# One-hots of q for a sort's lookups: TensorE transposes, or a VectorE comparison on bytes spread by DMA

## The chip, the cores and the metric

The kernel runs on one core of one Trainium2 chip. The metric is the device time of one execution in microseconds (us): less is better. Engines: PE is TensorE (PEld its weight loads), DVE is VectorE, ACT is ScalarE, POOL is GpSimd, SP is SyncE; a "q" behind a name (SPq) is the engine's queue.

## The reference

Two graph layers over 3,125 nodes of 128 features and 100,000 edges, with float32 in and out:

```
# layer 0: every edge sends h[dst] + edge_attr @ W_edge + b_edge to node src
h    = x @ W_lin + b_lin
aggr = segment_sum(h[dst] + (edge_attr @ W_edge + b_edge), src, 3125)
x    = layernorm(x + relu(aggr))
# layers of the second block, three times: mean over the edges of one (dst, type), 8 types
msg  = u[src];  seg = dst * 8 + type
h    = segment_sum(msg, seg) / max(count(seg), 1)
u    = einsum('nrf,rfo->no', h.reshape(n, 8, f), W) + u @ root + bias     # relu between them
out  = layernorm(x + u)
```

In the kernel the message of the second block is made at the edge's source and added at its destination. For that the edges are brought into an order by cells: a cell is a pair of q (the window of 128 destination nodes and the upper two bits of the type: Q = 100 values) and f (the source window and the type's last bit: F = 50 values).

## The kernel before

The stages, with their places in the profiled execution:

- 0 to 105 us: edges are loaded as a tile of 128 partitions x COLS = 784 columns. DVE and PE work out for each edge a row in DRAM (`slot_rows`), sorted by the window of src.
- 105 to 314 us: a histogram of the cells. DVE makes one-hots of q and f (`pick_qf`, L1232 in `pick_of`), PE multiplies them (`count_group`), and DVE turns the counts into start positions of the cells.
- 314 to 1356 us: the sort. 49 groups of GC = 16 columns (GROUPS = 49), each of GB = 4 steps of four columns; 196 steps. Two more groups only place.
- From about 1356 us: gathers, window sums, and the three layers. The change doesn't touch them.

Beside the first stages and most of the sort POOL scatters the edge rows to DRAM: EC = 98 chunks of CH = 8 indirect DMAs, 784 in all (L609). ACT builds each chunk in one of NB = 4 buffers (`build_rows`: it waits until the chunk four before has been scattered and landed). LEAD = 18 chunks are built ahead of the sort; then ACT builds two at the start of each of the first BUILDS = 40 groups (g0 from 0 to 39 in `rank_group`). The order on each engine is written out by hand, and engines meet only in semaphores.

One step n of the sort (column c of four; `sort_group` on PE, `rank_group` on ACT, `sort_picks` on DVE):

- PE, `turn_q(n + 1)`: four transposes of the q one-hots of the next step into the PSUM tile `QT` (100 x 512, float16; L895), then four of the 13 key bits into `BITS_T` (L897).
- ACT, `copy_bits` and `copy_q`: these two tiles go to SBUF, q as float32 into `pick_qT`, double buffered. All ACT copies have line L644.
- PE, for each column: `permute` of an older column (two matmuls of 500 columns, L806), then `look_up` (L809): the turned one-hot `pick_qT` picks from `table` (100 x 50, float32) the next free position of each edge's cell, and an `add` counts the column in. ACT copies the new table to SBUF for the next column (`copy_table`): a chain from PE to ACT and back, four times in a step.
- PE, `pair_keys(n + 1)`: which edges of a column have the same key (L904 and four L806); ACT `copy_same` takes it.
- DVE: `pick_place` makes four one-hots of 1000 (L1416; eight buffers, so it waits for the permute eight columns back), `take_looked(n - 1)` (L1386) takes what was looked up, `place` works out positions, and `pick_ranked` and `pick_dst` make the next group's one-hots (L1232).

`q_h` holds the q of each edge as float16 (128 partitions x 784 columns). What `look_up` needs turned is, for each of four columns, a 100 x 128 matrix with a one where q of the edge in that partition equals the row.

```
            def turn_q(n, par, c0):
                wait_used(pe, S["q_copied"], n)
                for c in range(4):
                    nc.tensor.transpose(QT[:, P * c:P * (c + 1)], column(pick_q[par], c0 + c), ident_h[:, :])
```

Of the kernel before, what the change touches and what calls it, by code (L numbers as in the profile page):

```python
# [24 lines left out]
F32 = mybir.dt.float32  # L25
F16 = mybir.dt.float16
BF16 = mybir.dt.bfloat16
I32 = mybir.dt.int32
# [5 lines left out]
P = 128  # L34
# [9 lines left out]
def ds(start, size):  # L44
    return bass.ds(start, size)


def gnn_resnorm(nc, x, src, dst, edge_attr, edge_type, W_lin, b_lin, W_edge, b_edge, W1, root1, b1,
# [62 lines left out]
    with ctx:  # L111
# [8 lines left out]
        slot_rows = nc.dram_tensor("slot_rows", [SLOTS + NW * P + COLS, PAY], F32).ap()  # L120
        slot_blocks = slot_rows.rearrange("(b r) f -> b (r f)", r=P // ZB)
        msgs = nc.dram_tensor("msgs", [SLOTS_A, D], F32).ap()
        msg_blocks = msgs.rearrange("(b k) f -> b (k f)", k=BLK)
# [79 lines left out]
        more_hi = [words(y_sb, at + b * HI // 2, HI // 2, BF16) for b in range(4)]  # L203
        at += 2 * HI
        pairs_at = 2 * HALF - 2 * P
        block_j, block_r = words(y_sb, pairs_at - 2 * NS, NS), words(y_sb, pairs_at - NS, NS)
# [54 lines left out]
        def take(size, dt=F32):  # L261
# [71 lines left out]
        DVE_BANKS = ACC // 2 + 1  # L333
        QT = ps[0:Q, 4, 0:256].bitcast(F16)
        BITS_T = ps[0:KEYBITS, 4, 256:512].bitcast(F16)
# [12 lines left out]
                 "qf_picked d_picked turned_q bits_copied q_copied paired same_made looked_up "  # L348
                 "column_counted table_copied mult_made columns_used lo_picked hi_picked perm_used "
                 "sort_done slots_made slots_used idx_made "  # L350
# [9 lines left out]
        gathered = [[sem(f"gathered{i}_{half}") for half in range(2)] for i in range(NB)]  # L360
        stored = [sem(f"stored{i}") for i in range(4)]
        b_gathered = [sem(f"b_gathered{i}") for i in range(RB)]

# [275 lines left out]
        def _(act):  # L639
# [33 lines left out]

            def copy_q(n, q):
                copy(pick_qT[:, q, :], QT).then_inc(S["q_copied"], 1)

# [4 lines left out]
            def rank_group(g, par, pair, g0):  # L681
                if g0 < BUILDS:
                    for q in range(2):
                        turn = LEAD + 2 * par + q
                        build_rows(2 * g + (LEAD + q), q, g + LEAD // 2, turn % NB, pair + turn // NB)
                for b in range(GB):
                    n = GB * g + b
                    ahead = g0 < GROUPS - 1 or b < GB - 1
                    copy_table(4 * n, 0)
                    if ahead:  # L690
                        copy_bits(n + 1, (b + 1) % 2)
                    copy_table(4 * n + 1, 1)
                    if ahead:
                        copy_q(n + 1, (b + 1) % 2)
                    copy_table(4 * n + 2, 0)
                    copy_table(4 * n + 3, 1)
                    if ahead:
                        copy_same(n + 1, (b + 1) % 2)

            copy_bits(0, 0)  # L700
            copy_q(0, 0)
            copy_same(0, 0)
# [88 lines left out]
        def _(pe):  # L791
# [55 lines left out]

            clear((2,))

            def count_group(g, par, n):  # L850
# [23 lines left out]
            for rh in range(BLK):  # L874
# [3 lines left out]
                m.then_inc(S["a_counted"], 1)  # L878
            pe.wait_ge(S["b_started"], 1)
            whole(ps[:, 4, 0:NS], ones[0:Q, :], started_b).then_inc(S["b_counted"], 1)  # L880
            for f in range(F):
# [10 lines left out]
            def turn_q(n, par, c0):  # L892
                wait_used(pe, S["q_copied"], n)
                for c in range(4):
                    nc.tensor.transpose(QT[:, P * c:P * (c + 1)], column(pick_q[par], c0 + c), ident_h[:, :])  # L895
                for c in range(4):
                    m = nc.tensor.transpose(BITS_T[:, P * c:P * (c + 1)], bits_st[:, par, c0 + c, :],  # L897
                                            ident_h[:, :])
                m.then_inc(S["turned_q"], 1)
# [204 lines left out]
        def _(dve):  # L1104
# [115 lines left out]
            bits(key2[:, :], raw[:, 2, :], 1, ALU.arith_shift_right)  # L1220
            then(v.scalar_tensor_tensor(q_h[:, :], key[:, :], 4.0, key2[:, :], ALU.mult, ALU.add))
            bits(key2[:, :], raw[:, 2, :], 1, ALU.bitwise_and)
# [15 lines left out]
            def pick_qf(g, par, done):  # L1238
                pick_of(pick_q[par], in_pairs(q_h[:, ds(g * GC, GC)]), Q)
                pick_of(pick_f[par][:, :, 0:F, :], in_pairs(f_h[:, ds(g * GC, GC)]), F).then_inc(S[done], 1)  # L1240

            def pick_hist(g, par, n):
# [134 lines left out]
            def pick_dst(g, par, half):  # L1377
# [3 lines left out]
                if half:  # L1381
                    m.then_inc(S["d_picked"], 1)

            def take_looked(n, b, par):
                dve.wait_ge(S["looked_up"], n + 1)
# [33 lines left out]
            def sort_picks(g, par, pair, g0):  # L1419
                for b in range(GB):  # L1420
# [6 lines left out]
                    if b and g0 < GROUPS:  # L1427
                        take_looked(GB * g + (b - 1), b - 1, par)
                    if b == 0 and 1 <= g0 <= GROUPS:
                        place(g - 1, 1 - par)  # L1430
# [7 lines left out]
                    if b >= 2 and g0 < GROUPS - 1:  # L1438
                        pick_dst(g + 1, 1 - par, b - 2)

            pick_ranked(0, 0)
            for half in range(2):
# [216 lines left out]
```

## Time and profile before

| | |
|---|---|
| median of 3 runs | 4906.59 us (4905.39 to 4911.11) |
| the profiled execution: time | 4906.83 us |
| the profiled execution: span, first to last instruction | 4905.1 us |
| outside the span | 1.7 us |
| mean granted TensorE clock | 0.905 |
| busy, share of span | PE 82%, DVE 69%, POOL 49%, ACT 44% |

How the profile is read: busy times are sums over an execution in which the stages have different limits. "Idle before" is the time in which an engine waited just before an instruction, and the name behind the arrow is what it waited for. A granted clock of 1.00 is TensorE's full 2.4 GHz, 0.50 is 1.2 GHz. Durations of neighbouring instructions of one engine can overlap a little.

### The profile page before, as it was taken

Reading aid. Unit: us, or ns where it says so; the run is one execution under the profiler, and the core shown is the slowest. Engines: PE = TensorE matmul, PEld = TensorE weight load, DVE = VectorE, ACT = ScalarE, POOL = GpSimd, SP = SyncE. Lnnn points to the kernel's source line nnn. Section 1 sums busy time; section 2 is a strip of 40 time slices with the busy share of each in tenths; the row PEclk is TensorE's granted clock in tenths of the full one; section 3 lists DMA queues with packets and bytes.
Section 4 is the critical chain, followed back from the end, with each engine's and each line's share of the span. In section 5 each row is a group of like instructions: output and inputs, shape, how many; then the busy total and the mean of one; then the engine's idle time right before and its main releaser. Section 6 shows DMA issues by size and latency. Waiting matters only on the chain.

```text
span 4905.1 us, 118298 instructions
## 1 busy us (share of the span) xinstructions
PE 3998.8 (82%) x30835; PEld 3134.4 (64%) x30836; DVE 3368.4 (69%) x8053; ACT 2159.3 (44%) x5004; POOL 2391.5 (49%) x2369
## 2 busy tenths in 40 slices
PE   3589888889956666666688889989889999888997
PEld 2456655656645554455457777776777776777776
DVE  8858777778877777777656665665665765666666
ACT  0025555555511111111145556765555775555675
POOL 2877777776067777777500005750002772000575
PEclk9559989889977888888789999999999999999999
DMA  1111111111033333333315556754555773555676
GB/s 43 39 43 55 46 51 48 48 51 30 0 97 77 78 77 77 78 77 76 51 43 171 170 170 188 208 169 124 172 172 168 208 209 103 172 172 172 189 209 180
DMA packets 672517, 553.37 MB, mean 113 GB/s; under 512 B 158723, under 2 KB 584885, under 8 KB 672462
## 3 DMA queue, kind: packets, MB, share of 16 engines
q0 software_dynamic: 111712, 277.47, 20.3%
q1 hardware_dynamic: 560750, 275.24, 19.3%
q8 instruction: 25, 0.41, 0.0%
q14 instruction: 30, 0.25, 0.0%
HBM read 307.55 MB, written 244.94 MB: 113 GB/s over the span
## 4 chain that ended last, share of the span: by engine, by line
PE 49%; POOL 24%; issue 16%; DVE 5%; DMA 5%; DVEq 1%; ACT 1%; POOLq 0%; ACTq 0%; SPq 0%
PE ps L809 25%; PE ps L806 17%; POOL slot_rows L609 11%; POOL y_sb L620 10%; PE ps L1065 4%; DMA mid<-msgs,block_idx 3%; POOL mid L632 3%; DMA y_sb<-in_x_dram,idx_st 1%; DVE mid L1531 1%; DVE y_sb L1262 0%; PE ps L897 0%; DVE y_sb L1232 0%; PE ps L1031 0%; DVE mid L1605 0%; PE ps L895 0%
## 5 line engine op out<-in xcount | busy, mean ns | idle before, releaser
L632 POOL DMA_INDIRECT mid<-msgs,block_idx x750 | 715.4, 954 | 1745.2 <-DMA msgs<-mid 1498.6
L644 ACT ACTIVATE mid<-ps 128x512 f32<-128x512 f16 (+4 forms) x2484 | 1083.8, 464 | 1023.1 <-PE ps L1065 298.9
L806 PE MATMUL ps<-mid 128*128 128x128 f32 (+3 forms) x7668 | 1236.1, 300 | 88.7 <-DMA mid<-msgs,block_idx 31.6
L806 PEld LDWEIGHTS ps<-mid 128*128 128x128 f32 (+3 forms) x7668 | 857.5, 175 | 318.7 <-issue 263.9
L809 PE MATMUL ps<-y_sb,mid 128*128 x6552 | 946.4, 288 | 132.8 <-issue 130.4
L620 POOL DMA_INDIRECT y_sb<-in_x_dram,idx_st x808 | 795.3, 984 | 413.3 <-issue 246.4
L609 POOL DMA_INDIRECT slot_rows<-y_sb,row_st x784 | 863.2, 1101 | 270.5 <-issue 236.9
L809 PEld LDWEIGHTS ps<-y_sb,mid 128*128 128x128 f32 x6552 | 794.7, 191 | 258.7 <-issue 211.7
L1605 DVE TENSOR_SCALAR mid<-iota,slot_lo,slot_w 128x128 f32<-128x128 f32 x2250 | 663.1, 378 | 313.9 <-PE ps L806 304.1
L809 PE MATMUL ps<-y_sb 128*128 128x193 f32 x1616 | 423.5, 417 | 291.3 <-DVE mid L1531 187.3
L644 ACT ACTIVATE y_sb<-ps 128x512 bf16<-128x512 f16 (+2 forms) x375 | 205.0, 554 | 1007.1 <-PE ps L986 877.2
L1596 DVE COPY mid<-ps 128x512 f32<-128x512 f32 x411 | 284.9, 693 | 482.2 <-PE ps L809 482.2
L809 PEld LDWEIGHTS ps<-mid 100*128 100x128 f32 (+2 forms) x1884 | 351.4, 208 | 388.7 <-ACT mid L644 213.7
L809 PE MATMUL ps<-mid 100*128 100x50 f32 (+2 forms) x1884 | 444.7, 329 | 145.8 <-ACT mid L644 90.0
L809 PEld LDWEIGHTS ps<-y_sb 128*128 128x128 f32 x1616 | 346.9, 244 | 310.9 <-DVE mid L1531 240.4
L1588 DVE TENSOR_TENSOR mid<-iota_h,a_code 128x512 f16<-128x512 f16 x819 | 525.6, 684 | 0.0
L806 PE MATMUL ps<-y_sb 128*100 128x50 f16 (+2 forms) x3886 | 494.8, 250 | 12.6 <-DVE y_sb L1232 12.6
L644 ACT ACTIVATE mid<-zeros,slot_w 128x128 f32<-128x128 f32 x750 | 371.2, 495 | 205.1 <-PE ps L806 168.4
L1531 DVE TENSOR_TENSOR mid<-mid,ps 128x193 f32 x808 | 286.8, 355 | 199.1 <-PE ps L809 71.2
L644 ACT ACTIVATE zeros<-iota,zeros 128x128 f32<-128x128 f32 x750 | 300.8, 401 | 106.2 <-DMA msgs<-mid 11.5
L1416 DVE TENSOR_SCALAR mid<-iota_h,mid 128x1000 bf16<-128x1000 f16 x392 | 213.0, 562 | 161.6 <-PE ps L806 159.1
L1065 PE MATMUL ps<-ident_h,mid 128*128 128x128 f16 x3276 | 318.0, 220 | 4.8 <-DVE mid L1588 4.6
(244 smaller groups left out, 3743.5 us busy)
## 6 DMA issues: line engine op xcount, KB each, us to landing
msgs<-mid SPq DMA_DIRECT2D x819, 256.0 KB, 2.3
y_sb<-slot_rows SPq DMA_DIRECT2D x101, 268.0 KB
y_sb<-in_edge_attr_dram SPq DMA_DIRECT2D x54, 256.0 KB
y_sb<-in_x_dram,idx_st POOLq DMA_INDIRECT x808, 2.5
slot_rows<-y_sb,row_st POOLq DMA_INDIRECT x784
mid<-msgs,block_idx POOLq DMA_INDIRECT x750, 3.7
y_sb<-in_edge_attr_dram SPq DMA_DIRECT2D x44, 224.0 KB
mid<-in_L_gnn_W_dram SPq DMA_DIRECT2D x3, 512.0 KB
```

The costliest lines, as they stand in the source:

```text
L609: nc.gpsimd.indirect_dma_start(out=slot_rows, out_offset=bass.IndirectOffsetOnAxis(ap=row_st[:, b, k:k + 1], axis=0), in_=stage[:, b, PAY ...
L620: nc.gpsimd.indirect_dma_start(out=slots[b][:, k, 0:D], out_offset=None, in_=x, in_offset=bass.IndirectOffsetOnAxis(ap=idx_st[:, b, k:k + ...
L632: nc.gpsimd.indirect_dma_start(out=rows[:, s % RB, :], out_offset=None, in_=msg_blocks, in_offset=bass.IndirectOffsetOnAxis(ap=block_idx[: ...
L644: return nc.scalar.activation(o, i, func, **kw)
L806: return nc.tensor.matmul(o, a, b, start=False, stop=False, skip_group_check=True)
L809: return nc.tensor.matmul(o, a, b, start=True, stop=True, skip_group_check=True)
L1065: t = nc.tensor.transpose(A_TRN[par][:, P * k:P * (k + 1)], a_sel[:, b, k, :], ident_h[:, :])
L1416: v.tensor_scalar(pick_hi[ci % 8], iota_h[:, 0:HI], hi_f[:, par, ci:ci + 1], mult[:, ds(c, 1)], ALU.is_equal, ALU.mult).then_inc(S["hi_pic ...
L1531: v.tensor_tensor(to, to, ps[:, (k // 2) % 2, SUM * (k % 2):SUM * (k % 2 + 1)], ALU.add).then_inc(S["tile_added"], 1)
L1588: v.tensor_tensor(a_sel[:, b, :, :], iota1_h[:, :].unsqueeze(1).to_broadcast([P, BLK, P]), a_code[:, ds(g * BLK, BLK)].unsqueeze(2).to_bro ...
L1596: v.tensor_copy(a_out[:, b, :], ps[:, 2 + b, :]).then_inc(S["a_taken_dve"], 1)
L1605: m = v.tensor_scalar(b_sel[:, b % 2, k, :], iota[:, 0:P], slot_lo[:, ds(s * BLK + k, 1)], slot_w[:, ds(s * BLK + k, 1)], ALU.is_equal, AL ...
```

## The change

The turned one-hots `pick_qT` are no longer made by PE and copied by ACT, but compared by DVE.

- Once, ahead of the histogram: PE transposes all of `q_h` in seven transposes (`Q_TURNED`, PSUM bank 4), DVE writes it as bytes (`q_st`) in two instructions, and ACT stores it to a DRAM tensor `q_codes`, one row of 128 bytes for each column of edges.
- For each step: ACT issues one DMA (`load_q`) that reads the 512 bytes of the step's four columns and writes them to each of 100 partitions (`q_row`, four buffers, issued three steps ahead, in the place in ACT's order where `copy_q` stood).
- For each step: DVE (`turned_q`, behind `take_looked`) compares the 100 x 512 bytes with the partition's number and writes `pick_qT` as float32.
- PE's transposes of q in `turn_q` and ACT's `copy_q` go. `turn_q` waits for `bits_copied` in place of `q_copied`.

```diff
+        q_codes = nc.dram_tensor("q_codes", [QTILES * P, P], U8).ap()
+        q_steps = q_codes[0:COLS, :].rearrange("(n i) p -> n (i p)", i=4)
...
-            def copy_q(n, q):
-                copy(pick_qT[:, q, :], QT).then_inc(S["q_copied"], 1)
+            def load_q(n, b):
+
+                wait_used(act, S["q_copied"], n - 3)
+                act.dma_start(q_row[b], q_steps[ds(n, 1), :].to_broadcast([Q, 4 * P])).then_inc(q_in[b], 16)
...
                     copy_table(4 * n + 1, 1)
-                    if ahead:
-                        copy_q(n + 1, (b + 1) % 2)
+                    if g0 < GROUPS - 1 or b < GB - 3:
+                        load_q(n + 3, (b + 3) % 4)
                     copy_table(4 * n + 2, 0)
...
+            act.wait_ge(S["q_staged"], 2)
+            act.dma_start(q_codes[0:(QTILES - 1) * P, :].rearrange("(t c) p -> c t p", c=P),
+                          q_st[:, 0:(QTILES - 1) * P].rearrange("c (t p) -> c t p", p=P)).then_inc(S["q_stored"], 16)
...
+            act.wait_ge(S["q_stored"], 32)
+            for n in range(3):
+                load_q(n, n)
             copy_bits(0, 0)
-            copy_q(0, 0)
...
             clear((2,))
+            pe.wait_ge(S["q_coded"], 1)
+            for t in range(QTILES):
+                n = min(P, COLS - t * P)
+                m = nc.tensor.transpose(Q_TURNED[0:n, t * P:(t + 1) * P], q_h[:, t * P:t * P + n], ident_h[:, :])
+            m.then_inc(S["q_turned"], 1)
...
             def turn_q(n, par, c0):
-                wait_used(pe, S["q_copied"], n)
-                for c in range(4):
-                    nc.tensor.transpose(QT[:, P * c:P * (c + 1)], column(pick_q[par], c0 + c), ident_h[:, :])
+                wait_used(pe, S["bits_copied"], n)
...
+            dve.wait_ge(S["q_turned"], 1)
+            whole_q = (QTILES - 1) * P
+            v.tensor_scalar(q_st[:, 0:whole_q], Q_TURNED[:, 0:whole_q], 1.0, None, ALU.mult).then_inc(S["q_staged"], 1)
+            rest_q = (slice(0, COLS - whole_q), slice(whole_q, whole_q + P))
+            v.tensor_scalar(q_st[rest_q], Q_TURNED[rest_q], 1.0, None, ALU.mult).then_inc(S["q_staged"], 1)
...
+            def turned_q(n, b, turn):
+
+                wait_used(dve, S["looked_up"], n - 1)
+                dve.wait_ge(q_in[b], 16 * turn + 16)
+                v.tensor_scalar(pick_qT[:, b % 2, :], q_row[b], part[0:Q, 0:1], None, ALU.is_equal
+                                ).then_inc(S["q_copied"], 1)
...
                         take_looked(GB * g + (b - 1), b - 1, par)
+                    if g0 < GROUPS - 1 or (g0 < GROUPS and b < GB - 1):
+                        turned_q(GB * g + (b + 1), (b + 1) % 4, g + (b + 1) // 4)
...
+            turned_q(0, 0, 0)
             pick_ranked(0, 0)
```

## Rows read from the trace of the kernel before

**Rows 1.** The page: the chain that ended last, by engine.
```profile
PE 49%; POOL 24%; issue 16%; DVE 5%; DMA 5%; DVEq 1%; ACT 1%; POOLq 0%; ACTq 0%; SPq 0%
```
**Rows 2.** The chain of waits in time, 300 to 1360 us: shares by line.
```profile
by line: POOL slot_rows L609 51.6%; issue 16.6%; PE ps L806 16.6%; PE ps L809 6.4%; PE ps L897 1.9%; PE ps L895 1.7%; PE ps L904 1.5%; ACT mid L644 0.5%; ACT y_sb L644 0.5%; PE ps L802 0.4%; POOLq L606 0.2%; POOLq L396 0.2%; DMA slot_rows<-
```
**Rows 3.** Windows of the sort: length, busy PE, PEld, DVE, ACT, POOL (xcount), PE clock, DMA.
```profile
450.00:700.00 250.00, 221.87 (x2089) 149.94 (x2088) 191.33 (x384) 129.57 (x392) 194.52 (x183) 0.90 0.17 48
1166.00:1183.40 17.40, 16.88 (x144) 11.65 (x144) 11.79 (x21) 8.83 (x28) 13.74 (x13) 0.80 0.09 26
1183.40:1200.70 17.30, 17.30 (x182) 11.87 (x180) 16.22 (x34) 9.77 (x29) 13.64 (x13) 1.00 0.08 24
1218.00:1322.00 104.00, 104.00 (x1080) 71.69 (x1080) 93.15 (x199) 58.94 (x168) 0.00 (x0) 1.00 0.00 0
```
**Rows 4.** ACT's wait for the chunk four before, at a group's start (timeline).
```profile
1165.53 0.75 ACT L644 ACTIVATE y_sb<-y_sb 128x512 f32<-128x512 f32 x2 [4.01 <-DMA slot_rows<-y_sb,row_st]
```
**Rows 5.** DVE's waits (total us, times, longest) and `copy_q`, 1218 to 1322 us.
```profile
DVE y_sb L1416 <- PE ps L806: 5.7, 12, 0.8
DVE mid L1416 <- PE ps L806: 4.3, 18, 0.4
L644 ACT ACTIVATE mid<-ps 100x512 f32<-100x512 f16 x24 | 14.2, 591 | 0.0
```
**Rows 6.** The timeline of one step at full clock: start, us, engine, line.
```profile
604.25 0.41 PE L895 MATMUL ps<-ident_h,y_sb 128*100 128x128 f16 x4
604.59 0.39 PE L897 MATMUL ps<-ident_h,y_sb 128*13 128x128 f16 x4
605.02 1.68 ACT L644 ACTIVATE mid<-ps 13x512 f16<-13x512 f16 x4 [0.55 <-PE ps L897]
607.24 0.41 PEld L809 LDWEIGHTS ps<-mid 100*128 100x128 f32 x2
```
**Rows 7.** DVE, lines by form, 0 to 320 us: forms near the added ones.
```profile
L1343 DVE TENSOR_SCALAR mid<-iota,mid 100x128 f32<-100x128 f32 x50 | 15.0, 299 | 16.0 <-PE ps L806 16.0
L1194 DVE TENSOR_SCALAR mid<-mid,start_col 25x808 f32<-25x808 f32 x1 | 0.6, 629 | 0.0
L1252 DVE TENSOR_SCALAR mid<-mid 128x784 int32<-128x784 int32 x1 | 0.6, 569 | 0.0
L1187 DVE TENSOR_SCALAR mid<-ps 128x784 int32<-128x784 f32 x1 | 1.0, 976 | 1.5 <-PE ps L806 1.5
```
**Rows 8.** Scatters of POOL beside DVE instructions (timeline).
```profile
196.28 1.31 POOL L609 DMA_INDIRECT slot_rows<-y_sb,row_st  x1 [0.30 <-issue]
262.90 0.29 DVE L1343 TENSOR_SCALAR mid<-iota,mid 100x128 f32<-100x128 f32 x1 [0.48 <-PE ps L806]
263.09 0.97 POOL L609 DMA_INDIRECT slot_rows<-y_sb,row_st  x1 [0.30 <-issue]
263.10 0.41 DVE L1344 TENSOR_SCALAR mid<-mid 100x250 f32<-100x250 f32 x1
605.12 1.21 DVE L1232 TENSOR_TENSOR y_sb<-y_sb,mid 128x2048 f16<-128x2048 f16 x1
605.61 1.56 POOL L609 DMA_INDIRECT slot_rows<-y_sb,row_st  x1 [0.30 <-issue]
```
**Rows 9.** The start of the histogram and of the sort (timeline).
```profile
110.11 2.97 PE L806 MATMUL ps<-y_sb 128*100 128x50 f16 x32 [5.63 <-DVE y_sb L1232]
318.06 0.63 PE L895 MATMUL ps<-ident_h,y_sb 128*100 128x128 f16 x4
319.26 1.06 ACT L644 ACTIVATE mid<-ps 13x512 f16<-13x512 f16 x2 [39.04 <-PE ps L897]
323.31 0.97 POOL L609 DMA_INDIRECT slot_rows<-y_sb,row_st  x1 [3.94 <-ACT row_st L644]
```
**Rows 10.** Issues on SP's queue (timeline), and a time to landing (DMA view).
```profile
322.67 1.09 SPq L493 DMA_DIRECT2D y_sb<-in_edge_attr_dram  x2
...
slot_rows<-zeros SPq DMA_DIRECT2D x1, 871.0 KB, 6.1
```

More of the change, by code:

```diff
@@ L26 @@
 F16 = mybir.dt.float16
+U8 = mybir.dt.uint8
 BF16 = mybir.dt.bfloat16
@@ L121, in gnn_resnorm @@
         slot_blocks = slot_rows.rearrange("(b r) f -> b (r f)", r=P // ZB)
+        QTILES = -(-COLS // P)
+        q_codes = nc.dram_tensor("q_codes", [QTILES * P, P], U8).ap()
+        q_steps = q_codes[0:COLS, :].rearrange("(n i) p -> n (i p)", i=4)
         msgs = nc.dram_tensor("msgs", [SLOTS_A, D], F32).ap()
@@ L204, in gnn_resnorm @@
         at += 2 * HI
+        q_at = COLS * KEYBITS // 2 + COLS // 2
+        q_row = [words(y_sb, q_at + b * P, P)[0:Q, :].bitcast(U8) for b in range(4)]
+        q_st = words(y_sb, q_at + 4 * P, QTILES * P // 4).bitcast(U8)
+        assert q_at + 4 * P + QTILES * P // 4 <= SORT_AT
         pairs_at = 2 * HALF - 2 * P
@@ L333, in gnn_resnorm @@
         DVE_BANKS = ACC // 2 + 1
-        QT = ps[0:Q, 4, 0:256].bitcast(F16)
+        Q_TURNED = ps[:, 4, 0:QTILES * P // 2].bitcast(F16)
         BITS_T = ps[0:KEYBITS, 4, 256:512].bitcast(F16)
@@ L348, in gnn_resnorm @@
                  "qf_picked d_picked turned_q bits_copied q_copied paired same_made looked_up "
-                 "column_counted table_copied mult_made columns_used lo_picked hi_picked perm_used "
+                 "q_coded q_turned q_staged q_stored column_counted table_copied mult_made columns_used lo_picked hi_picked perm_used "
                  "sort_done slots_made slots_used idx_made "
@@ L361, in gnn_resnorm @@
         stored = [sem(f"stored{i}") for i in range(4)]
+        q_in = [sem(f"q_in{i}") for i in range(4)]
         b_gathered = [sem(f"b_gathered{i}") for i in range(RB)]
@@ L698, in rank_group @@
                         copy_same(n + 1, (b + 1) % 2)
+            act.wait_ge(S["q_staged"], 2)
+            act.dma_start(q_codes[0:(QTILES - 1) * P, :].rearrange("(t c) p -> c t p", c=P),
+                          q_st[:, 0:(QTILES - 1) * P].rearrange("c (t p) -> c t p", p=P)).then_inc(S["q_stored"], 16)
+            rest = COLS - (QTILES - 1) * P
+            act.dma_start(q_codes[COLS - rest:COLS, :], q_st[0:rest, (QTILES - 1) * P:QTILES * P]
+                          ).then_inc(S["q_stored"], 16)
+            act.wait_ge(S["q_stored"], 32)
+            for n in range(3):
+                load_q(n, n)
             copy_bits(0, 0)
-            copy_q(0, 0)
             copy_same(0, 0)
@@ L879, in _ @@
             pe.wait_ge(S["b_started"], 1)
+            pe.wait_ge(S["q_staged"], 2)
             whole(ps[:, 4, 0:NS], ones[0:Q, :], started_b).then_inc(S["b_counted"], 1)
@@ L1220, in _ @@
             bits(key2[:, :], raw[:, 2, :], 1, ALU.arith_shift_right)
-            then(v.scalar_tensor_tensor(q_h[:, :], key[:, :], 4.0, key2[:, :], ALU.mult, ALU.add))
+            v.scalar_tensor_tensor(q_h[:, :], key[:, :], 4.0, key2[:, :], ALU.mult, ALU.add).then_inc(S["q_coded"], 1)
+            dve.wait_ge(S["q_coded"], 1)
             bits(key2[:, :], raw[:, 2, :], 1, ALU.bitwise_and)
```

## The prediction

> **What bounds the kernel now.** I began with the chain that ended last: PE 49%, POOL 24% [rows 1]. The change touches one stage of it, so the next view was the chain in time over the sort: the scatters of L609 carry 51.6% of it, and most of the 16.6% "issue" is the gap of 0.30 us behind each of them [rows 2, 8]. PE stands there with under 30%. The windows tell where. From 450 to 700 us POOL is busy for 194.52 of 250 us with 183 scatters, so one comes every 1.366 us and the 16 that belong to a group take 21.9 us; PE has its clock at 0.90 [rows 3]. At a group's start ACT waits up to 4.01 us for a chunk that POOL has only just scattered, and everyone behind ACT waits with it [rows 4]. The last such wait ends at 1165.53. From there on PE is the bound: 104.00 us busy of 104.00, at full clock, and `copy_q`, which runs once a step, has run 24 times: 4.333 us a step, 17.33 a group [rows 3, 5]. So a group costs PE 17.33 us, and in the first 40 groups POOL needs more than that. What the sort's engines gain there is waited away; a gain on PE counts in group 39 and in the nine behind it.
>
> And DVE is close behind PE: in the same 104 us it waited for PE only 5.7 + 4.3 = 10.0 us, 0.417 a step [rows 5]. Its own work, gaps and overlaps counted, is 4.333 - 0.417 = **3.916 us a step**.
>
> **What goes.** The four q transposes of a step take PE from 604.25 to 604.59: 0.34 us at full clock [rows 6], about 0.6 at half clock (0.63 at 318.06) [rows 9]. PE alone would then step in 3.99 us. ACT's copy of q is one of the four in the 1.68 us behind `copy_bits` [rows 6]. It delays nobody today: the third table copy ends with that row at 606.70, and PE loads for that lookup at 607.24. So its going brings nothing.
>
> **What comes on DVE.** `turned_q` is a compare with a per-partition scalar, 100 x 512, float32 out, 196 times. The trace has no byte input. Nearest is L1343 (100 x 128, the same compare, float32): 0.299 us in the mean; L1194 has 808 elements in 0.629 [rows 7]. The slope is 0.330/680 = 0.485 ns an element, so 512 give 0.299 + 384 x 0.000485 = 0.485 us. Neighbours on DVE overlap (L1343 starts at 262.90, lasts 0.29, and the next starts at 263.10) [rows 8] by 0.09, so it takes 0.40 us of DVE's time. The other end is half that rate: of the same 784 elements, L1187 takes 0.976 us where L1252 takes 0.569, 0.52 ns more an element [rows 7]; for 512 that gives 0.75 us, 0.67 of DVE's time. I take 0.40, since L1343 does the same operation with the same output. By the Trainium skill (VectorE: DVE Perf Modes, "What auto-detection actually checks") a single source with source and target in SBUF gets two elements a cycle whatever the type; no row here shows it for bytes.
>
> DVE's step becomes 3.916 + 0.40 = **4.316 us**, against PE's 3.99 and today's 4.333. The bound moves from PE to DVE and the step stays as it is. This is the core of the forecast. Its two new waits hold nothing: `looked_up` was just waited for by `take_looked`, and the bytes were asked for three steps ahead, 13 us, where 871 KB land in 6.1 us [rows 10]. If they did hold, `pick_ranked` and the one-hots for `permute` stand behind them on DVE, and PE waits for those. PE's own wait for `pick_qT` has slack: DVE makes it right behind `take_looked`, whose wait ends as PE starts the step before the one that needs it.
>
> **What comes on ACT.** One DMA issue a step in the place of a copy. Two issues on SP's queue with an address from a register took 1.09 us, 0.55 each [rows 10]; the copy took 0.591 [rows 5]. Up to 0.54 us more than the copy (from 606.70 to 607.24), that is to about 1.1 us, the issue delays nobody.
>
> **Start.** DVE's byte writes stand ahead of the histogram, which DVE paces: L1187 (PSUM, 784 elements) took 0.976 [rows 7], so 768 take about 0.96, the 16 x 128 rest 0.29, less overlap: +1.1 us (at two elements a cycle +0.7). PE's seven transposes, some 1.1 us at half clock by 0.63 for four, lie in its wait of 5.63 us [rows 9]; without this cover they would cost that 1.1. Store and first loads lie in ACT's wait of 39.04 us, and POOL stands still for 3.94 us until the first chunk is built [rows 9], so a late sort start counts in full. On that path q's transposes at 318.06 go: -0.6. The first `turned_q` (0.4) is hidden: PE clears banks until 318.06 and comes to the one-hots only then [rows 9]. Start: **+0.5 us**.
>
> **Groups 0 to 38.** DVE's 1.6 us more and PE's 1.4 less a group both disappear in POOL's 21.9: **0**, if a scatter stays as long as it is.
>
> **Groups 39 to 48.** Group 39 starts at half clock with DVE rested (11.79 busy of 17.40) [rows 3]: PE's gain, 0.6 + 2 x 0.34, -1.3. In groups 40 and 41 POOL still runs and DVE is slower, 16.22 us busy in the first against 93.15/6 = 15.53 later [rows 3]: twice 17.26 + 0.69 - 17.33 at most, and less in the second: +1.1. Groups 42 to 47: 24 x -0.017 = -0.4. Group 48 has no next group's one-hots to make, so PE is the bound, with three sets of transposes less: -1.0. Sum **-1.6**; I add 1 us for hand-overs between two engines that are both about 90% busy or more.
>
> The sum: 4906.83 + 0.5 + 0 - 1.6 + 1.0 = 4906.7, **4907 us**. It is made against the profiled execution (span 4905.1 and 1.7 around it), which lies 0.2 us above the median.
>
> **Rivals.**
>
> *PE's gain is kept.* DVE's work with the compare stays under PE's 3.99 us a step, because its instructions run closer together when it never waits; of the 0.40 added only 3.99 - 3.916 = 0.07 may show. Then groups 40 to 48 run at 3.99: 35 x 0.34 = 11.9, against nothing in the forecast but group 48's 1.0 and the 0.7 around it. 4906.83 + 0.5 - 1.3 - 11.9 = 4894. Against it: DVE is 90% busy already [rows 3], and the smaller compare L1343 alone takes 0.299. For it: DVE's 3.916 us are worked out from waits, not from rows of each gap.
>
> *POOL's scatters get longer (slower).* Place: the 156 steps of the POOL-bound groups 0 to 38. A scatter takes 0.97 alone, but 1.56 where an L1232 of 1.21 us (two SBUF inputs) covers its start, and 1.31 beside float and integer instructions of 0.57 us [rows 8]. `turned_q` stands between L1386 and, in three steps of four, an L1232. If it costs a scatter half of 0.34 us, that is 156 x 0.17 = 27: 4934. It decides from 0.063 us each (9.8/156). Against it: beside L1343 and L1344, which share operation, scalar and output type with it, the scatter at 263.09 stays at 0.97 [rows 8]. The Trainium skill (GPSIMD Engine Reference, "Key points") says that VectorE instructions in a two-port mode contend with GpSimd for SBUF; L1343 at two elements a cycle would be one, and that scatter doesn't show it; the one at 605.61, under a two-input L1232, does. The order in time of scatters and L1232 shifts too, either way: a scatter takes 194.52/183 = 1.063 in the mean, 0.09 over 0.97, some 56 us in 39 groups of 16, and a tenth of it is 6.
>
> *A byte costs one element a cycle.* DVE's step is 3.916 + 0.67 = 4.586, 0.253 over today's in 32 steps: +8.1. With +1.1, +0.5, -1.3 and 1 for hand-overs: 4916.
>
> *The bytes come late or ACT's issue exceeds 1.1 us*, so that lookups wait: the change then isn't the prefetch it says. At 1.5 us an issue PE would step in 4.4: +3 over ten groups, inside the forecast's range.
>
> **How the numbers follow.** The forecast, with the last rival in it: 0.57, its own range 4899 to 4917 (6 us for the scatters' order, 2 for the start, 2 for hand-overs, either way). PE's gain kept: 0.16. Scatters longer: 0.17. Bytes at one a cycle: 0.10. The range leaves out most of the scatters' rival and a little on the fast side: 4892 to 4926. A measurement of this kernel can tell 0.2%, 9.8 us, from no change. Faster by more: 0.16 and a tail of 0.01, 0.17. Slower: 0.15, 0.05 of the byte rival and 0.02: 0.22. Between: 0.61.
>
> **What the profile after would show.** Right: in the window of the last groups DVE without waits and PE with some 0.3 us of idle a step; steps of 4.3 us; scatters' mean between 1.05 and 1.09; the last of ACT's waits for a chunk ending within 8 us of 1165.5. Wrong: `turned_q` far from 0.48 us; scatters of 1.2 us beside it; DVE's waits for PE as before; PE's clock below 1.00 in the last groups.

## The result

The changed kernel takes 5018.95 us (median of 4 runs, 5015.75 to 5022.51), the kernel before 4908.85 in the same runs: a ratio of 1.0226, 95% interval 1.0213 to 1.0239. The forecast was 4907, its range ended at 4926, so it missed by 112 us. The profiled execution has a span of 5020.8 us, 115.7 over the span before.

Scatters over the whole profile, first before (L609) and then after (L618): count, busy us, mean ns, idle before them.

```profile
L609 POOL DMA_INDIRECT slot_rows<-y_sb,row_st x784 | 863.2, 1101 | 270.5 <-issue 236.9
```
```profile
L618 POOL DMA_INDIRECT slot_rows<-y_sb,row_st x784 | 1004.0, 1281 | 263.9 <-issue 237.5
```

The same 784 scatters, with the same gap of 0.30 us behind each (236.9 and 237.5 us of "issue" in all), are busy for 140.8 us more. The windows after show where; the first answers the first of [rows 3], the second the last of [rows 3] (columns as there).

```profile
450.00:700.00 250.00, 191.56 (x1612) 128.48 (x1610) 172.54 (x366) 91.47 (x296) 201.84 (x159) 0.82 0.18 51
...
1333.00:1437.00 104.00, 102.95 (x1026) 68.54 (x1025) 103.39 (x230) 49.19 (x151) 9.10 (x5) 1.00 0.06 14
```

In 250 us POOL gets through 159 scatters instead of 183, so one comes every 1.572 us where it was 1.366, and a group of 16 takes 25.2 us, not 21.9. PE does less in that time and its granted clock is 0.82 instead of 0.90. In the last groups it is as forecast: DVE, busy for 103.39 of 104 us, is the bound, and PE has idle time at full clock.

ACT's last wait for a chunk, which ended at 1165.53 [rows 4], now ends here:

```profile
1289.68 0.75 ACT L653 ACTIVATE y_sb<-y_sb 128x512 f32<-128x512 f32 x2 [4.66 <-DMA slot_rows<-y_sb,row_st]
```

That is 124.2 us later. The sort's result is copied out at 1472.3 where it was 1356.0, 116.3 us later. So all of the loss, and 7.9 us more, arises in the groups that POOL bounds, and the last groups give 7.9 back.

**One scatter.** The timeline of DVE and POOL in step 1 of a group, before (start, us, engine, line):

```profile
709.26 1.22 DVE L1232 TENSOR_TENSOR mid<-y_sb,mid 128x2048 bf16<-128x2048 f16 x1
709.46 1.85 POOL L609 DMA_INDIRECT slot_rows<-y_sb,row_st  x1 [0.30 <-issue]
710.39 0.21 DVE L1374 COPY y_sb<-y_sb 128x208 f16 x1
710.51 1.47 DVE L1232 TENSOR_TENSOR y_sb<-y_sb,mid 128x1600 f16<-128x1600 f16 x2
711.62 1.21 POOL L609 DMA_INDIRECT slot_rows<-y_sb,row_st  x1 [0.30 <-issue]
```

The scatter ends at 711.31, 0.83 us behind the end of the first one-hots (710.48), though the copy and two more follow: at that boundary it got in. The same place after:

```profile
616.15 0.37 DVE L1423 TENSOR_TENSOR mid<-ps,y_sb 128x204 f32<-128x204 f32 x1
616.44 0.48 DVE L1418 TENSOR_SCALAR mid<-y_sb,part 100x512 f32<-100x512 uint8 x1
616.83 1.22 DVE L1256 TENSOR_TENSOR mid<-y_sb,mid 128x2048 bf16<-128x2048 f16 x1
616.94 3.46 POOL L618 DMA_INDIRECT slot_rows<-y_sb,row_st  x1 [0.30 <-issue]
617.96 0.21 DVE L1404 COPY y_sb<-y_sb 128x208 f16 x1
618.09 1.47 DVE L1256 TENSOR_TENSOR y_sb<-y_sb,mid 128x1600 f16<-128x1600 f16 x2
```

Here it ends at 620.40, 0.84 us behind the end of the *last* one-hots (619.56). It was kept out through the whole chain: one-hots of the low digit, copy of the bits, one-hots of q and f. A third scatter, in steps 2 and 3, where no chain follows:

```profile
622.11 1.21 DVE L1256 TENSOR_TENSOR y_sb<-y_sb,mid 128x2048 f16<-128x2048 f16 x1
622.20 1.96 POOL L618 DMA_INDIRECT slot_rows<-y_sb,row_st  x1 [0.30 <-issue]
```

It started 0.09 us behind the one-hots and took 1.96; the one at 605.61 started 0.49 behind them and took 1.56 [rows 8]. Both end 0.84 us after the one-hots do. The 0.40 us between them are what the compare moved the one-hots by.

So there are two effects, and I have taken the sum over all scatters from 323 us to the last one (640 single ones before, 641 after), each less 0.967, a free one's duration. Before, 69.7 us; after, 206.1.

- 42 scatters take more than 2.25 us, 99.9 us over a free one in all, 2.38 each. Before there is none; at 0.60 each (the mean of those of 1.4 to 2.25 us before) they would be 25. The chains' hold: 75 us.
- 78 take 1.4 to 2.25 us, 0.99 each over a free one, against 0.60: 30 us.
- Together that is 120 scatters held by one-hots, before it was 71: 49 more, at 0.60: 29 us. The rest is 2.

What holds them was open here: the compare, the loads, or the order of things.

### The profile page after: what moved, and what is told of

The parts are those of the page before. It is cut to its first block, busy times and chain, and to the rows that moved or that the text cites. A ratio compares the mean times of both kernels' runs of the same rounds, so it can differ in the third digit from the quotient of the medians.

```text
span 5020.8 us, 117371 instructions
## 1 busy us (share of the span) xinstructions
PE 3976.7 (79%) x30058; PEld 3110.5 (62%) x30059; DVE 3424.7 (68%) x8251; ACT 2064.4 (41%) x4808; POOL 2532.2 (50%) x2369
## 4 chain that ended last, share of the span: by engine, by line
PE 45%; POOL 27%; issue 16%; DMA 5%; DVE 5%; DVEq 1%; ACT 0%; POOLq 0%; SPq 0%; ACTq 0%
PE ps L828 24%; PE ps L825 15%; POOL slot_rows L618 15%; POOL y_sb L629 10%; DMA mid<-msgs,block_idx 4%; PE ps L1088 4%; POOL mid L641 2%; DMA y_sb<-in_x_dram,idx_st 1%; DVE mid L1645 0%; DVE y_sb L1292 0%; DVE mid L1571 0%; DVE y_sb L1256 0%; PE ps L1054 0%; PE ps L1107 0%; DVE y_sb L1532 0%
## 5 line engine op out<-in xcount | busy, mean ns | idle before, releaser
L653 ACT ACTIVATE mid<-ps 128x512 f32<-128x512 f16 (+4 forms) x2288 | 988.1, 453 | 1123.7 <-PE ps L825 450.2
L825 PE MATMUL ps<-mid 128*128 128x128 f32 (+3 forms) x7668 | 1257.0, 303 | 92.1 <-DMA mid<-msgs,block_idx 33.8
L618 POOL DMA_INDIRECT slot_rows<-y_sb,row_st x784 | 1004.0, 1281 | 263.9 <-issue 237.5
L828 PEld LDWEIGHTS ps<-mid 100*128 100x128 f32 (+2 forms) x1884 | 374.3, 220 | 520.1 <-ACT mid L653 331.0
L828 PE MATMUL ps<-mid 100*128 100x50 f32 (+2 forms) x1884 | 457.5, 337 | 266.5 <-ACT mid L653 209.7
L828 PEld LDWEIGHTS ps<-y_sb 128*128 128x128 f32 x1616 | 335.1, 236 | 321.8 <-DVE mid L1571 239.6
L1453 DVE TENSOR_SCALAR mid<-iota_h,mid 128x1000 bf16<-128x1000 f16 x392 | 207.1, 563 | 270.3 <-PE ps L825 268.7
```

What stands on the lines that cost most here:

```text
L618: nc.gpsimd.indirect_dma_start(out=slot_rows, out_offset=bass.IndirectOffsetOnAxis(ap=row_st[:, b, k:k + 1], axis=0), in_=stage[:, b, PAY ...
L653: return nc.scalar.activation(o, i, func, **kw)
L825: return nc.tensor.matmul(o, a, b, start=False, stop=False, skip_group_check=True)
L828: return nc.tensor.matmul(o, a, b, start=True, stop=True, skip_group_check=True)
L1453: v.tensor_scalar(pick_hi[ci % 8], iota_h[:, 0:HI], hi_f[:, par, ci:ci + 1], mult[:, ds(c, 1)], ALU.is_equal, ALU.mult).then_inc(S["hi_pic ...
```

## The experiments

Each time is compared with that of the kernel before, run beside it. The changed kernel, f1, i1 and i2 ran 4, 4, 4 and 10 times; the others ran once, so 10 us mean little there. The scatter columns are made as above, from 323 us on.

```
kernel                            us over before  scatters over 2.25 us  sum over free us
before                                   0                0                    70
changed                               +110               42                   206
e1 loads only                         +100                0                   130
e2 compare only                       +115               43                   205
e3 compare before take_looked          +94               41                   179
e4 compare last in the step           +147               94                   268
f1 float16 for bytes                  +111               43                   204
f4 nothing turns q                      +3                0                    87
g4 before + a met wait                  +2                0                    70
g2 before + copy 128 x 16              +30                0                    98
g1 before + compare 128 x 16           +54               13                   123
h1 before + copy 100 x 16              +72               41                   144
f3 before + compare 100 x 16           +74               41                   152
f2 before + byte compare 100 x 16      +80               41                   154
g3 before + two compares 100 x 16      +92               41                   165
h2 changed, compare on 128             +48                0                   135
h3 changed, chain split                +40                2                   124
h4 before, chain split                  -6                0                    71
i1 changed, 128, compare last          +28                0                   116
i2 changed, 128, last, chain split       0                0                    82
```

**Loads or compare (e1, e2).** e1 keeps staging, store and loads and turns q as before:

```diff
+                    if ahead:
+                        copy_q(n + 1, (b + 1) % 2)
                     if g0 < GROUPS - 1 or b < GB - 3:
                         load_q(...)
```


> Everything of the change but the compare: the bytes are staged, stored and loaded each step as in the changed kernel, but nobody compares them; PE turns the one-hots of q and ACT copies them, as in the kernel before. The output stays the reference's. Theory A (the compare on VectorE is what holds GpSimd's scatters): scatters stay at 1.10 us in the mean, about 4909 us. Theory B (the per-step loads crowd the scatters, by their issue or their traffic): scatters at 1.28 us, about 5019 us; ACT has a copy and an issue in one step here, 0.3 us more than in the changed kernel, which nobody should wait for.

e2 drops the loads of each step (`load_q` only four times at the start).

> Everything of the change but the loads of each step: the bytes of the first four steps are loaded once, and all 196 compares read these four buffers, so the one-hots of q from step 4 on are those of other steps and the output is not the reference's; instructions of all engines but ACT's issues are those of the changed kernel. Theory A (the compare): scatters 1.28 us in the mean, about 5019 us. Theory B (the loads): scatters 1.10 us, about 4900 to 4909 us. If both have a part, the time lies between, and with the run that has the loads alone it should add up to 110 us.

e2 took 5018.95 us, the time of the changed kernel: the 193 loads and issues in the steps are worth nothing. But e1 took 5004.04, which looks like the opposite. Its trace says why it was a bad experiment. The timeline of ACT in one of its last steps:

```profile
1342.33 1.42 ACT L656 ACTIVATE mid<-ps 13x512 f16<-13x512 f16 x3 [1.24 <-PE ps L931]
1343.25 0.29 ACTq L693 DMA_DIRECT2D y_sb<-q_codes  x1
1343.80 0.21 ACT L656 ACTIVATE mid<-ps 100x50 f32<-100x50 f32 x1
```

Copy of q *and* issue stand ahead of the third table copy, and PE's step is 5.03 us long (its transposes start at 1340.87 and at 1345.90) against 4.333. No scatter of e1's sort takes over 2.25 us. So part of its loss is a fault of its own; f4 is the clean version. But not all of it is that fault: its last scatter starts at 1278.7 where it was 1208.2, and 109 scatters take 1.4 to 2.25 us where 71 did, without a compare in the steps. The loads, or the longer steps of PE and ACT, moved the scatters by that much; which of the two isn't shown.

**Place (e3, e4).** `turned_q` moved ahead of `take_looked` (e3), or behind the one-hots as the last of a step (e4).

> The changed kernel with one thing moved: on VectorE the compare stands ahead of take_looked in each step and no longer directly ahead of the one-hots of two inputs. Theory A1 (a scatter that starts beside the compare is held through the compare and the two-input instructions right behind it; a PSUM-reading multiply between them lets it go): the 3.45 us scatters go, the mean returns to 1.10, about 4900 to 4910 us. Theory A2 (the place does not matter, the compare's own 0.47 us a step of port time does): 196 x 0.17 to 0.47 us more than before in any place, 5000 us or more.

> The changed kernel with the compare as the last instruction of each step on VectorE, behind the one-hots and ahead of the next step's four scalar compares. Theory A1 (it harms only directly ahead of the two-input one-hots): scatters 1.10 us in the mean and about 4900 to 4910 us, if PE does not wait for it. Theory A2 (its port time counts anywhere): 5000 us or more. Theory A3 (any two-port instructions in a row are one blocked stretch, and behind the one-hots the compare only lengthens that stretch by 0.47 us): scatters of 1.96 where they were 1.56, some 4930 to 4960 us.

4997.61 and 5050.70. A1 falls in both: a PSUM-reading multiply between compare and one-hots does not let the scatter in, and at the end of a step it is worst (94 long ones). A2 had set 5000 us or more for both, and e3 lies just under that; A3, 4930 to 4960 for e4, falls too. e4's long ones also show that two inputs aren't needed to keep a scatter out: 93 of the 94 end 0.11 to 0.12 us behind one of `pick_place`'s one-hots (L1453, 128 x 1000, one input), which follow the compare there. I had taken the compare's place for the cause.

**Bytes, and nothing at all (f1 to f4).** In e1, too, a scatter was held for 3.33 us, once, behind the byte writes of the start. So I suspected the bytes.

> The changed kernel with q's values kept as float16 instead of bytes, from the staging through the store and the loads to the compare: same instructions in the same places, 100 KB a load instead of 50. The traces so far show chains of two-input one-hots that keep a scatter out from end to end (3.45 us) only where an instruction with bytes ran right ahead of them: the byte writes at the start (3.33 us, also in the kernel with the loads alone, against 1.67 before) and the byte compare. Theory C (the byte is what closes the boundaries between VectorE's instructions): scatters fall back to about 1.1 us, the compare stays at 0.47 us or less, and the gain at the end is kept: 4895 to 4915 us. Theory D (any compare in this place shifts the one-hots by 0.4 us and holds the scatters so): 5019 us again, scatters 1.28 us.

f1 has float16 in `q_codes`, `q_row` and `q_st`. Result 5018.39, ratio 1.0224 (1.0207 to 1.0241): the bytes are innocent. f2 and f3 put a small compare into the kernel before. This is f3's; f2's reads 16 bytes as its source, `iota[0:Q, 0:4].bitcast(U8)`:

```diff
+                    if g0 < GROUPS - 1 or (g0 < GROUPS and b < GB - 1):
+                        wait_used(dve, S["extra_made"], GB * g + (b - 3))
+                        v.tensor_scalar(extra[0:Q, b, :], iota[0:Q, 0:16], part[0:Q, 0:1], None, ALU.is_equal
+                                        ).then_inc(S["extra_made"], 1)
```


> The kernel before, with one small instruction added to each step on VectorE in the place of the compare: 100 x 16 bytes compared, into a buffer that nobody reads. It shifts the one-hots by 0.05 to 0.1 us instead of 0.4. Theory C (the byte): scatters of 3.3 us and more where a chain of one-hots follows, 4960 us or more. Theory D (the shift by the compare's length): under 4930 us.

> The same small instruction with a float32 source of 100 x 16. Theory C: as the kernel before, within 15 us of it. Theory D: the same as the run with the small byte instruction, whatever that is. A rival to C, that it is the 100 partitions or the scalar from memory and not the byte: as the run with the small byte instruction too, and slow.

4986.51 and 4980.53: an instruction of 0.23 us that nobody reads costs 80 and 74 us. f3 has no byte in it, so theory C falls. Nor is it the length, which was theory D. The timeline of f3:

```profile
834.63 0.23 DVE L1434 TENSOR_SCALAR y_sb<-iota,part 100x16 f32<-100x16 f32 x1
834.77 1.22 DVE L1235 TENSOR_TENSOR mid<-y_sb,mid 128x2048 bf16<-128x2048 f16 x1
835.16 3.18 POOL L612 DMA_INDIRECT slot_rows<-y_sb,row_st  x1 [0.30 <-issue]
```

The scatter starts 0.39 us behind the one-hots, a place from which every scatter got in at the first boundary before. And with q turned by nobody:

> The changed kernel without its 194 later loads and compares: the one-hots of q are made for two steps at the start and read by all, so nothing turns q any more on PE, ACT or VectorE, and the output is not the reference's. All theories that put the loss on the compare: scatters 1.10 us in the mean, the sort's last groups at PE's own step of 3.99 us, about 4895 us. A theory that puts it on the sort's order without q's transposes (PE or ACT earlier, phases shifted): 4950 us or more.

4909.63, no long scatter. e2, with the compares and without the loads of the steps, took 5018.95; f4 has neither. So the compare is the cause. But the time is 15 us over what I expected: in the last groups PE steps in 3.99 us (100 one-hots of `pick_place` in the 99.7 us from 1239.6 to 1339.3), which brings 9.3 us, and the last scatter starts at 1221.4 instead of 1208.2, because scatters take 17 us more in sum. With no compare in the steps, that shift comes with less work on PE and ACT, and it eats the gain.

**What trait of the instruction (g1 to g4, h1).** The small instruction of f3, varied: on all 128 partitions (g1); `tensor_copy` on 128 (g2); two of f3's in a row (g3); the wait without an instruction (g4); `tensor_copy` on 100 partitions (h1).

> The kernel before with the small float compare in each step (100 x 16, it cost 77 us), now on all 128 partitions. Theory E (an instruction on fewer than 128 partitions is what makes the chain behind it keep scatters out): within 15 us of the kernel before. If the number of partitions has nothing to do with it: again 70 to 85 us over before, with scatters of 3.4 us.

> The same with a plain copy of 128 x 16 float32 in the place of the small compare. Theory F (a compare, or a scalar from memory, is what matters): within 15 us of before. Theory G (any VectorE instruction in this place does it, because the one-hots are queued behind it and then run without a gap that a scatter could enter): 60 to 85 us over before, scatters of 3.4 us beside the chain of three one-hots.

> Two of the small compares in a row in each step. Theory G: as with one, 70 to 95 us over before, since one is enough to close the gap. Theory H (what counts is on which turn, of two, an instruction falls, so that one more shifts the turn and two shift it back): near the kernel before, within 25 us. If each small instruction simply costs its own blocking: twice 77, some 155 us.

> No instruction added, only the register update and a semaphore wait that is always met, in the place of the compare. All theories that put the loss on an instruction of VectorE's data path: within 15 us of before. If it is VectorE's instruction stream (one more register update and wait behind take_looked): 70 to 85 us over.

> The kernel before with a plain copy of 16 elements in each step in the compare's place, on 100 partitions (on 128 it cost 30 us and no chain kept a scatter out; the small compare on 100 partitions cost 76, with every chain keeping it out). Theory E (fewer than 128 partitions is what does it): 65 to 85 us over before, with scatters of 2.5 to 3.5 us. Theory I (the tensor-scalar form does it): 20 to 40 us over, no scatter above 2.0 us.

4958.55, 4934.57, 4996.93, 4906.53 and 4978.60. A wait costs nothing. Two are not a second time 77, and they don't restore anything. g2 and h1 differ in the number of partitions alone. The timeline of g2, then of h1:

```profile
698.62 0.17 DVE L1434 COPY y_sb<-iota 128x16 f32<-128x16 f32 x1
698.70 1.22 DVE L1235 TENSOR_TENSOR mid<-y_sb,mid 128x2048 bf16<-128x2048 f16 x1
698.82 1.93 POOL L612 DMA_INDIRECT slot_rows<-y_sb,row_st  x1 [0.30 <-issue]
699.83 0.21 DVE L1377 COPY y_sb<-y_sb 128x208 f16 x1
699.95 1.47 DVE L1235 TENSOR_TENSOR y_sb<-y_sb,mid 128x1600 f16<-128x1600 f16 x2
701.05 1.21 POOL L612 DMA_INDIRECT slot_rows<-y_sb,row_st  x1 [0.30 <-issue]
```
```profile
669.00 0.18 DVE L1434 COPY y_sb<-iota 100x16 f32<-100x16 f32 x1
669.07 1.22 DVE L1235 TENSOR_TENSOR mid<-y_sb,mid 128x2048 bf16<-128x2048 f16 x1
669.51 3.13 POOL L612 DMA_INDIRECT slot_rows<-y_sb,row_st  x1 [0.31 <-issue]
670.21 0.21 DVE L1377 COPY y_sb<-y_sb 128x208 f16 x1
670.33 1.47 DVE L1235 TENSOR_TENSOR y_sb<-y_sb,mid 128x1600 f16<-128x1600 f16 x2
```

A copy of 0.17 or 0.18 us in both. Behind the one on 128 partitions the scatter is let in at the first boundary (0.83 us after 699.92), behind the one on 100 only at the end of the chain (0.84 after 671.80). In all of g2 no scatter takes over 2.25 us, in h1 41 do, one in nearly every group. g1 is a miss for theory E, which had said within 15 us: on 128 partitions it has 13 long scatters where f3 has 41, and costs 54 us. And g2's 30 us are neither F's nor G's.

**In the change itself (h2, h3, h4).** h2:

```diff
-                v.tensor_scalar(pick_qT[:, b % 2, :], q_row[b], part[0:Q, 0:1], None, ALU.is_equal
+                v.tensor_scalar(all_qT[:, b % 2, :], q_row[b], part[:, 0:1], None, ALU.is_equal
```


> The changed kernel with loads and compare on all 128 partitions instead of 100 (rows 100 to 127 are never read). Theory E: the chain lets scatters in as before, what is left is the shift of the one-hots by 0.4 us, so scatters of 1.96 and no 3.45: a gain of 1.5 us in each of 39 groups, some 4960 us. Theory I: 5019 us again.

4954.39, 6 us from what theory E said. Its step 1 in the timeline:

```profile
662.06 0.48 DVE L1419 TENSOR_SCALAR mid<-y_sb,part 128x512 f32<-128x512 uint8 x1
662.45 1.22 DVE L1257 TENSOR_TENSOR mid<-y_sb,mid 128x2048 bf16<-128x2048 f16 x1
662.58 1.93 POOL L619 DMA_INDIRECT slot_rows<-y_sb,row_st  x1 [0.30 <-issue]
...
663.71 1.47 DVE L1257 TENSOR_TENSOR y_sb<-y_sb,mid 128x1600 f16<-128x1600 f16 x2
```

1.93 us where it was 3.46, from almost the same start (0.13 and 0.11 behind the one-hots). What is left of the loss, 48 us, I put down to the second effect, that the compare in front delays the one-hots; i1 tests it.

h3 and h4 move `pick_ranked` of the next group from step 1 to step 0, in the changed kernel and in the one before:

```diff
-                    if b == 1 and g0 < GROUPS - 1:
+                    if b == 0 and g0 < GROUPS - 1:
                         wait_used(dve, S["columns_used"], GB * g if g0 else 0)
                         pick_ranked(g + 1, 1 - par)
```


> The changed kernel with the copy of the bits and the one-hots of q and f for the next group moved from step 1 of a group to step 0, where they follow place() instead of the one-hots of the low digit; all instructions stay. Theory: the chain compare, one-hots, copy, one-hots, one-hots is what holds one scatter a group for 3.45 us; split in two it holds it for at most 1.5 + 0.85: some 1.1 us less a group, 40 us less in all, 4975 us; a rival, that what one chain loses the other place gets: 5010 us or more.

> The kernel before with the same move. There no chain held a scatter beyond its first one-hot, so a theory of the chain expects little from it: 4890 to 4920 us. If the scatters' phases against VectorE decide whatever the order, it may land anywhere within 4880 to 4950.

4946.11 and 4900.25. Splitting the chain takes 73 us from the changed kernel (I had expected 40) and leaves 2 scatters over 2.25 us, of 2.35 and 2.36; the kernel before, whose chain kept no scatter out beyond its first one-hots, moves by 6 us, which one run can't tell from nothing.

**Together (i1, i2).** Compare on 128 partitions and last in the step; i2 with the split too.

> The changed kernel with loads and compare on all 128 partitions and the compare as the last instruction of a step. On 100 partitions in this place it took 5051 us. Theory (partitions plus shift are all of it): the one-hots start where they did before the change, a scatter beside them takes 1.56 us again and none is held by a chain: scatters 1.08 to 1.11 us in the mean, the gain of 8 us at the end kept: 4893 to 4915 us. Rival (the compare's port time counts by itself too, since behind the one-hots it is one more instruction that a scatter can meet): 4930 us or more.

> The same with the next group's copy of bits and one-hots of q and f made in step 0 of a group, which saved 73 us in the changed kernel on 100 partitions and 6 in the kernel before. Theory: 0 to 10 us less than the run without the move, 4885 to 4910 us. Rival (with the compare in every step the scatters' phases decide, whatever the order): 4930 us or more.

i1: 4937.41, ratio 1.0066 (1.0048 to 1.0085). The rival holds: with the one-hots back at their place 28 of h2's 48 us remain, so their delay isn't all of the second effect. The timeline of a scatter beside one-hots in i1:

```profile
617.04 1.21 DVE L1257 TENSOR_TENSOR y_sb<-y_sb,mid 128x2048 f16<-128x2048 f16 x1
617.54 1.68 POOL L619 DMA_INDIRECT slot_rows<-y_sb,row_st  x1 [0.30 <-issue]
618.17 0.48 DVE L1419 TENSOR_SCALAR mid<-y_sb,part 128x512 f32<-128x512 uint8 x1
```

It starts 0.50 behind them, as at 605.61 [rows 8], but ends 0.97 behind their end, not 0.84: the compare behind them adds 0.13, and scatters that met the last one-hots of a chain and took 1.20 or 1.21 before take 1.31 to 1.33. i2: 4909.06 us for 4909.09, ratio 0.9998 (0.9988 to 1.0008), 10 and 13 runs. With partitions, place and chain put right the change costs nothing that these runs can tell, and brings nothing. No version beat the kernel before by more than this can tell.

## Why the prediction was wrong

**What held.** The compare: forecast 0.485 us, at two elements a cycle; measured (lines by form)

```profile
L1418 DVE TENSOR_SCALAR mid<-y_sb,part 100x512 f32<-100x512 uint8 x196 | 93.3, 476 | 0.1
```

The row agrees with the Trainium skill (VectorE: DVE Perf Modes, "What auto-detection actually checks") on bytes too. The rival of one element a cycle, which had put it at 0.75 us, is gone. The bytes came in time (DVE was idle for 0.1 us in all before the 196 compares), and ACT's issue took 0.29 us, under the 1.1 that were allowed. The start: the byte writes took 0.96 and 0.27 and the first histogram matmul came 0.93 us later, but POOL restarted at 323.06 instead of 323.31 [rows 9], so it cost nothing where +0.5 was forecast. In the last groups DVE is the bound.

**The step that failed** is "Groups 0 to 38: 0, if a scatter stays as long as it is". The condition stood there, and its breach was the second rival, at 0.17 and 27 us. Its place and its sign were right, and its mechanism, that the compare keeps scatters waiting, in part; its price was wrong by a factor of five. Over the 156 steps of these groups the scatters grew by 136/156 = 0.87 us a step, not 0.17. Three things made the rival small:

- *The price.* "Half of 0.34" priced the compare as one more instruction that a scatter meets: 0.34 is what those of 0.57 us add. It harms mostly by what it does to the one-hots behind it: it moves them by 0.40 us, so that a scatter that begins beside them waits that much longer, and it makes a chain of them impassable, 2.38 us over a free scatter each time. Neither was in the sum.
- *The row against it.* The scatter at 263.09 beside L1343 stays at 0.97 [rows 8], but behind L1343 comes one short float32 instruction and then a wait for PE. In the sort the next instruction is 1.2 us of one-hots. The row had the right instruction in the wrong company. And the trace of before had dearer rows, which the forecast didn't weigh: from 199 to 230 us 12 scatters take 2.08 to 2.21 us beside a one-input instruction of 1.86 (L1262).
- *The spread.* I allowed 6 us for the scatters' order, a tenth of what they take over 0.97. It moved by far more than a tenth. Before, 71 scatters met one-hots; with the compare in front 120 did. One that has been let in at the end of a DVE instruction ends a fixed time later, and the next starts 0.30 us after that, so in step after step POOL meets DVE at the same place: 60 scatters of 1.9 to 2.0 us after, one or two in nearly every group, where 36 of 1.5 to 1.6 stood before. A shift of 0.4 us is then paid in nearly every group. g2 comes nearest to showing it alone: a copy of 0.17 us, behind which no chain keeps a scatter out, costs 30 us. That the fixed place is the reason is argued from these rows, not shown by a run of its own.

The Trainium skill (GPSIMD Engine Reference, "Key points") says that GpSimd contends for SBUF with VectorE instructions in a two-port mode or with two SBUF inputs. The one-hots that hold the scatters have two SBUF inputs, so the traces agree, and where the forecast weighed that rule it had the size wrong: 1 to 2.5 us on a scatter of 0.97.

**A term that was mis-sized.** DVE's step, forecast 4.316 us, is 4.13: 24 compares start from 1337.2 to 1432.2, 95.0/23. Less the compare's 0.40, DVE's own work is 3.73, not the 3.916 taken from its waits. So the first rival was half true: of PE's 0.34 us a step 0.20 is kept, and the last groups gave 7.9 us instead of the forecast's 0.6. PE's own step, 3.99, was right (f4).

**What stays open.** That an instruction on 100 partitions makes the chain behind it impassable is shown by g2 against h1 and by the change itself against h2. Why, it isn't; nor why the small compare on 128 partitions (g1) still did it 13 times. How far behind such an instruction the effect reaches is known in part: past a multiply that reads PSUM (e3), and at the start of the sort past a copy on 128 partitions, where a scatter at 315.67 took 4.54 us beside four one-hots. Not tried: 96 or 112 partitions.

## What to carry to other kernels

Where GpSimd sets the pace with short indirect DMAs, an instruction added to VectorE is not free because VectorE has time: look for what stands behind it, and at which phase the scatters meet that. Keep VectorE's instructions on all 128 partitions even where the data fills 100, and break chains of long instructions without a wait between them. A range of 20 us was too narrow for such a change from a trace of before; here a copy of 16 elements cost 30.

## What the runs showed of the hardware

- A copy of 16 elements a partition, 196 times: +30 us on 128 partitions, +72 on 100; the same semaphore traffic without it, +2.
- In the sort, a scatter held by two-input one-hots ends 0.83 to 0.85 us after them (all 71 of the kernel before), and 0.96 or 0.97 where the compare follows (i1). One held by one-input instructions ended 0.11 to 0.12 us after them (93 in e4, 12 before the sort in the kernel before).
- Behind an instruction on 100 partitions (16 at the start of the histogram, where one scatter took 3.33 us) a scatter was kept out of up to four two-input instructions in a row, and in e4 of four one-input ones; behind a copy or the 512-element compare on 128 partitions at most of one two-input instruction. The 16-element compare on 128 (g1) is the exception, 13 times.
- A compare of 512 elements with float32 output takes 477 ns from float16 (f1) and 476 from bytes, in the mean of 196.
- A dynamic DMA issue on ScalarE's queue took 0.29 us; on SyncE's queue two took 1.09 [rows 10].
